# Layer a prepared while e waits, f's rows over the bfloat16 parts, and 32x32 blocks inverted on GpSimd in a six-layer decoder

## The reference, cut to what matters

```
x = norm(x + a(x))          # layer norm, q/k/v, rotation, 1+s+s*s/2 in place of exp, 16 heads of 16
x = norm(x + b(x, ctx))     # attention on ctx, with mask, bias
x = norm(x + c(x))          # 8 experts, top 2, 256 -> 512 -> 256
x = norm(x + d(x))          # delta rule in chunks, two causal filters (3 and 31 taps), a gate, a mix of four
x = norm(x + e(x, ctx))     # attention, softmax, without projections
x = norm(x + f(x))          # 256 -> 704 -> 256, inputs and weights rounded to 4-bit values by blocks of 16
```

## Time and profile before

| | |
|---|---|
| median of 3 runs (3577.76 to 3584.74) | 3583.84 us |
| profiled execution, its own time | 3585.07 us |
| profiled execution, span from first to last instruction | 3582.9 us |
| TensorE busy (weight loads) | 3074.0 us (2306.0) |
| VectorE busy | 2406.8 us |
| ScalarE busy | 1390.2 us |
| GpSimd busy | 355.2 us |
| mean granted clock of TensorE, share of full speed | 0.91 |

### The profile page before, as it was taken

How to read it: one execution, slowest core, us unless ns; L and a number is a source line. 1 busy time by engine, 2 the same in 40 slices (tenths; PEclk the granted TensorE clock), 3 DMA queues, 4 the chain that set the end, 5 groups by cost and what they waited for, 6 DMA issues and landing times.

```text
span 3582.9 us, 49503 instructions
## 1 busy us (share of the span) xinstructions
PE 3074.0 (86%) x18500; PEld 2306.0 (64%) x18500; DVE 2406.8 (67%) x5671; ACT 1390.2 (39%) x2889; POOL 355.2 (10%) x710
## 2 busy tenths in 40 slices
PE   4688889899898989989898998989899898999664
PEld 2466757677575766767576676757667675777452
DVE  5526567585866758577685767768576776867764
ACT  2334343434343343434344443344444334342321
POOL 1002001010100101001010100101010010101200
PEclk7789999998999999899999999999999999999776
DMA  3434234233323433332333333233433333341201
GB/s 103 88 87 104 54 89 95 69 84 86 84 57 77 104 72 82 83 86 60 77 85 91 72 89 86 64 77 87 89 72 86 86 67 77 80 97 50 48 12 24
DMA packets 592812, 275.92 MB, mean 77 GB/s; under 512 B 464808, under 2 KB 555072, under 8 KB 592576
## 3 DMA queue, kind: packets, MB, share of 16 engines
q1 hardware_dynamic: 490176, 138.53, 20.5%
q10 hardware_dynamic: 102400, 134.23, 12.1%
HBM read 156.55 MB, written 14.68 MB: 48 GB/s over the span
## 4 chain that ended last, share of the span: by engine, by line
PE 52%; DVE 23%; ACT 8%; issue 6%; DMA 5%; SPq 3%; POOL 3%; DVEq 0%; ACTq 0%; POOLq 0%
PE bank L890 20%; PE bank L1094 7%; PE bank L965 5%; PE bank L942 5%; ACT pt_f L1354 3%; DVE region L1971 3%; SPq L696 3%; DMA qT_f<-rest_f 2%; DVE nm_f L1711 2%; PE bank L1255 2%; PE bank L925 2%; PE bank L1176 2%; DMA kT_f<-split_f 2%; ACT split_f L1365 2%; PE bank L957 1%
## 5 line engine op out<-in xcount | busy, mean ns | idle before, releaser
L1354 ACT ACTIVATE pt_f<-bank 128x512 f32<-128x512 f32 x768 | 417.4, 596 | 368.5 <-PE bank L942 366.0
L1094 PE MATMUL bank<-c_w,c_hb 128*128 128x256 f32 x2048 | 509.2, 395 | 1.6 <-ACT c_hb L1483 0.3
L890 PE MATMUL bank<-xTc,c_w 128*128 128x256 f32 x2048 | 498.3, 393 | 1.3
L1711 DVE TENSOR_REDUCE nm_f<-bank 128x2 f32<-128x512 f32 x512 | 315.4, 685 | 203.1 <-PE bank L925 202.3
L1094 PEld LDWEIGHTS bank<-c_w,c_hb 128*128 128x128 f32 x2048 | 393.0, 200 | 64.9 <-ACT c_hb L1483 8.9
L890 PEld LDWEIGHTS bank<-xTc,c_w 128*128 128x128 f32 x2048 | 387.7, 195 | 64.8 <-issue 6.0
L1971 DVE SCALAR_TENSOR_TENSOR region<-vpad,cols,region 128x256 f32<-128x256 f32 x1024 | 425.8, 490 | 0.0
L942 PE MATMUL bank<-qT_f,kT_f 102*128 102x256 bf16 (+1 forms) x1536 | 293.9, 310 | 108.8 <-ACT pt_f L1354 39.4
L1483 ACT ACTIVATE c_hb<-bank,cols 128x256 f32<-128x256 f32 x512 | 213.8, 471 | 328.1 <-PE bank L890 328.0
L942 PEld LDWEIGHTS bank<-qT_f,kT_f 102*128 102x128 bf16 (+1 forms) x1536 | 123.6, 103 | 290.5 <-ACT pt_f L1354 120.9
L965 PE MATMUL bank<-pt_f,v_f 128*32 128x256 f32 x3072 | 231.5, 428 | 0.0
(11 more groups left out here) (309 smaller groups left out, 5012.4 us busy)
## 6 DMA issues: line engine op xcount, KB each, us to landing
c_w<-in_c_w ACTq DMA_DIRECT2D x256, 512.0 KB, 4.9
gram_scratch<-region SPq DMA_DIRECT2D x32, 256.0 KB, 2.3
x<-in_x SPq DMA_DIRECT2D x16, 256.0 KB, 5.7
x<-in_ctx SPq DMA_DIRECT2D x16, 256.0 KB, 5.9
ctxb<-in_ctx SPq DMA_DIRECT2D x16, 256.0 KB, 2.8
out_dram<-x SPq DMA_DIRECT2D x16, 256.0 KB, 2.2
qT_f<-split_f SPq DMA_TRANSPOSE x192, 3.3
kT_f<-split_f SPq DMA_TRANSPOSE x192, 3.4
```

The source lines that it names most:

```text
L890: mm = pe.matmul(out_ap, l, r, start=(i == 0), stop=(i == len(pairs) - 1))
L1094: mm = pe.matmul(PS[use][:, t * D:(t + 1) * D], c_hb[:, k, t * P:(t + 1) * P], c_w2[:, e % W_SLOTS, k, :], start=(k == 0), stop=(k == HC - 1))
L1354: act.activation(dst, PS[use].rearrange("p (c s) -> p c s", c=c), func, **kw).then_inc(*PS.drained(use))
L1711: dve.tensor_reduce(a.nm[:, :, h], PS[use].rearrange("p (t s) -> p t s", t=T), AX.X, ALU.max, negate=True)\
```

## The change

BASE goes from 4 to 5: blocks of 32x32, four in a matrix, 32 partitions, 31 pairs of operations, and doubling levels 5 and 6 alone. The orders of all engines are written anew. In a full step, layer a's norm and projection come before e's maxima, its v projection and first scores right after e's, its scores stand between f's segments, and the first doubling product (now d_one5) comes after a_out and b_in. f's inner rows move from pt into the tile split, over the bfloat16 parts, and f restores the constant columns of split when it is done; hence new waits: ScalarE waits for e's transposes before a's copies and for a's before f's tanh, and VectorE for x2 before f_res. Layer a's turned input gets a place of its own (aT = yf), the divided heads and the row maxima (on, mT, m3) move into slots of pt, and bank uses follow the new order.

```diff
-BASE = 4
+BASE = 5
...
-CONSTANTS = 54 - 4 * (LEVELS - 2)
+CONSTANTS = 30
...
-ONE = (["e_in"] + E_
-
-       + ["a_norm", "e_res", "a_proj", "e_apply", "f_in", "a_rope", "f_up0", "a_part1", "f_up1", "a_part2", "a_turnq",
-          "f_round0", "a_turnk", "f_round1", "f_down", "f_res", "f_apply"]
-       + A_[4:] + ["b_in", "b_ctx", "a_res", "a_apply", "b_x", "b_proj"]
-       + attention_segments("b", True) + ["b_res", "b_apply"])
+B_ = attention_segments("b", True)
+ONE = """
+a_load e_in e_part1 e_part2 e_turnq e_turnk a_norm a_proj a_rope e_max0 e_max1 e_max2 e_max3 e_shift a_part1 e_again a_part2
+""".split() + E_[10:-1] + """
+a_v a_turnq a_turnk e_out e_res e_apply f_in a_score0a a_score0b f_up0 a_score1a a_score1b f_up1 a_weigh0 a_score2a a_score2b
+a_weigh1 a_score3a a_score3b f_round0 a_weigh2 a_weigh3 f_round1 a_out b_in b_ctx a_res a_apply f_down b_x f_res b_proj
+""".split() + B_[:2] + ["f_apply"] + B_[2:] + ["b_res", "b_apply"]
...
     ("sync", None, """
-e_in e_turnq e_turnk e_again a_norm a_turnq d_blocks d_fetch a_turnk d_place d_begin f_apply b_turnq b_turnk b_again
+a_load e_in e_turnq e_turnk a_norm e_again a_turnq a_turnk d_blocks d_fetch d_place d_begin f_apply b_turnq b_turnk
+b_again
...
     ("gpsimd", None, """
-d_norm a_norm d_blocks e_res d_solve0 d_solve1 d_solve2 d_solve3 f_res a_res d_out d_res c_res b_res
+a_norm d_norm d_blocks e_res d_solve0 d_solve1 d_solve2 d_solve3 a_res f_res d_out d_res c_res b_res
...
     ("gpsimd", 17, """
-d_norm d_blocks d_solve0 d_solve1 d_solve2 d_solve3 e_res d_out f_res d_res
+d_norm d_blocks d_solve0 e_res d_solve1 d_solve2 d_solve3 f_res d_out d_res
...
     ("tensor", None, """
-d_in c_in c_gate d_proj c_comb c_up0a c_up0b e_max0 e_max1 c_down0a e_max2 e_max3 c_down0b c_up1a e_again c_up1b
-c_down1a e_score0a e_score0b e_score1a e_score1b e_weigh0 e_score2a c_down1b e_score2b e_weigh1 e_score3a d_token
-e_score3b e_weigh2 e_weigh3 e_out c_up2a c_up2b a_norm c_down2a c_down2b a_proj f_in c_up3a f_up0 f_up1 c_up3b d_chan
-c_down3a c_down3b d_gram c_up4a c_up4b f_round0 c_down4a f_round1 d_grams f_down a_score0a a_score0b a_score1a
-a_score1b a_weigh0 a_score2a c_down4b a_score2b a_weigh1 a_score3a c_up5a a_score3b a_weigh2 a_weigh3 d_one4 a_out
-b_in d_two4 b_ctx a_res d_twb4 c_up5b d_one5 b_x d_two5 b_proj c_down5a d_twb5 d_one6 c_down5b d_two6 c_up6a d_scan0
...
+d_in c_in d_proj a_norm a_proj c_gate e_max0 c_comb e_max1 c_up0a e_max2 c_up0b e_max3 c_down0a c_down0b e_again
+c_up1a c_up1b e_score0a c_down1a e_score0b c_down1b e_score1a c_up2a e_score1b e_weigh0 e_score2a e_score2b e_weigh1
+e_score3a d_token e_score3b e_weigh2 e_weigh3 a_v e_out c_up2b d_chan c_down2a c_down2b d_gram c_up3a f_in a_score0a
+d_grams a_score0b c_up3b f_up0 a_score1a c_down3a a_score1b c_down3b f_up1 c_up4a a_weigh0 a_score2a c_up4b a_score2b
+a_weigh1 a_score3a c_down4a a_score3b c_down4b f_round0 a_weigh2 a_weigh3 f_round1 c_up5a a_out b_in d_one5 b_ctx
+d_two5 a_res d_twb5 f_down d_one6 b_x c_up5b b_proj d_two6 c_down5a c_down5b d_scan0 c_up6a d_scan1 d_scan2 d_scan3
...
     ("vector", None, """
...
+e_part1 e_part2 a_norm a_proj a_rope d_proj c_gate e_max0 c_comb e_max1 e_max2 e_max3 e_shift a_part1 c_down0b d_conv
+d_silu d_token a_part2 c_down1b d_norm e_out e_res e_apply f_in d_gram c_down2b d_grams d_fir0 f_up0 d_fir1 d_fir2
+f_up1 c_down3b f_round0 f_round1 d_fir3 d_fir4 c_down4b d_one5 a_out d_fir5 d_two5 b_ctx a_res d_twb5 a_apply d_fir6
+f_res b_proj b_part1 b_part2 f_apply d_sums d_turn c_down5b b_max0 b_max1 b_max2 b_max3 b_shift c_down6b d_logit
...
-        low = region[0:P // 2, 2048:3072]
-        blkX, blkT, blkU = (low[:, i * 256:(i + 1) * 256].rearrange("p (r c) -> p r c", r=BB) for i in range(3))
-        blkT2 = low[:, 256:768]
-        blk_tmp = low[:, 768:832]
...
+        BN = 8 * NBK
+        square = lambda x: x[0:BN, 0:BB * BB].rearrange("p (r c) -> p r c", r=BB)
+        blkT, blkX = square(region[:, 2048:3072]), square(region[:, 3072 + 7 * 512:3072 + 9 * 512])
+        blkU = blkX
+        blk_tmp = wTn[0:BN].rearrange("p a s -> p (a s)")
...
-        f_h = flat_pt[:, 0:T * FF].rearrange("p (t n) -> p t n", t=T)
...
+        flat_split = at_.split[:, :, :, :, :].rearrange("p t i h x -> p (t i h x)").bitcast(F32)
+        f_h = flat_split[:, 0:T * FF].rearrange("p (t n) -> p t n", t=T)
...
                 for j in range(BB - 1):
-                    if j % 4 == 0:
-                        yield f"d_solve{j // 4}"
+                    if j % 8 == 0:
+                        yield f"d_solve{j // 8}"
...
                 act.wait_ge(*att["a"]["src"](b))
+                if b >= LAG["e"]:
+                    for half in range(HALVES):
+                        act.wait_ge(*att["e"][f"turned{half}"](b - LAG["e"]))
...
                     yield f"f_up{t}"
+                    if t == 0:
+                        if b + LAG["f"] < NB:
+                            for half in range(HALVES):
+                                act.wait_ge(*att["a"][f"turned{half}"](b + LAG["f"]))
...
                 yield "f_res"
+                if b + LAG["f"] < NB:
+                    dve.wait_ge(*xo["x2_ready"](b + LAG["f"]))
                 residual(b, "f_y", yf, x6)
+                dve.memset(a.split[:, :, 0, :, MASK0:MASK0 + 3], 1.0)
+                dve.memset(a.split[:, :, 0, :, MAX0:MAX0 + 3], 0.0)
+                dve.memset(a.split[:, :, :, :, SLOT:PITCH], 0.0)
+                dve.memset(a.split[:, :, 1, :, MAX0:MAX0 + 3], 1.0)
```

More of the change, by code:

```diff
@@ L155 @@
+a_weigh2 a_weigh3 a_out b_in b_ctx a_res b_x b_proj w_turn0 w_turn1 w_turn2 w_turn3 b_max0 b_max1 b_max2 b_max3
 b_again b_score0a b_score0b b_score1a b_score1b b_weigh0 b_score2a b_score2b b_weigh1 b_score3a b_score3b b_weigh2
@@ L192 @@
[L192 to L195 removed]
+e_part1 d_in e_part2 a_rope d_proj c_in c_gate c_comb c_up0a c_up0b a_part1 e_again a_part2 c_up1a c_up1b e_score0a
@@ L228 @@
-a_norm e_res a_proj e_apply f_in a_rope c_down2b d_norm d_gram f_up0 a_part1 f_up1 a_part2 f_round0 c_down3b f_round1
-d_grams d_fir0 d_fir1 f_res d_fir2 d_fir3 f_apply d_one4 d_fir4 a_out d_two4 b_ctx c_down4b a_res d_twb4 a_apply
-d_one5 d_fir5 b_proj d_two5 b_part1 d_twb5 b_part2 d_fir6 c_down5b b_max0 d_sums b_max1 b_max2 d_turn b_max3 b_shift
-c_down6b d_logit d_weight d_mix d_ms d_out d_res d_apply b_out c_down7b c_res c_apply b_res b_apply
+e_part1 e_part2 a_norm a_proj a_rope d_proj c_gate e_max0 c_comb e_max1 e_max2 e_max3 e_shift a_part1 c_down0b d_conv
@@ L257 @@
-f_up1 f_round0 d_turn f_round1 d_logit d_weight d_mix d_ms d_out f_res f_apply d_res d_apply
+e_part1 e_part2 d_proj d_conv d_silu d_token e_max0 d_norm e_max1 e_max2 e_max3 e_shift d_gram d_grams d_fir0 d_fir1
+d_fir2 d_fir3 e_out e_res e_apply f_in d_fir4 f_up0 f_up1 f_round0 f_round1 d_one5 d_fir5 d_two5 d_twb5 d_fir6 d_sums
+f_res f_apply d_turn d_logit d_weight d_mix d_ms d_out d_res d_apply
 """),
@@ L339, in at, with maxima, scores, turned_up @@
         u.extend((segment, use, bank) for use, bank in uses)
-    def attention(l, again):
-        if again:
-            for g in range(4):
-                at(f"{l}_max{g}", *((f"{l}_m{h}", h % 4) for h in range(4 * g, 4 * g + 4)))
-            at(f"{l}_again", (f"{l}_rT", 0))
-        for g in range(5):
-            if g < 4:
-                at(f"{l}_score{g}", *((f"{l}_s{h}", h % 2) for h in range(4 * g, 4 * g + 4)))
-            if g == 1 and not again:
-                at(f"{l}_weigh0", (f"{l}_sv", 3))
-            if g in (1, 3):
-                at(f"{l}_weigh{g - 1}", (f"{l}_o{g // 2}", 2 + g // 2))
-        at(f"{l}_out", (f"{l}_ot0", 0), (f"{l}_ot1", 1))
-    attention("e", True)
-    at("a_norm", ("a_hT", 2))
-    at("a_proj", ("a_qk0", 3), ("a_qk1", 0), ("a_v", 1))
-    at("f_in", ("f_xT", 2))
-    for t in range(T):
-        at(f"f_up{t}", (f"f_g{t}a", 0), (f"f_g{t}b", 1), (f"f_u{t}a", 2), (f"f_u{t}b", 3))
-    for t in range(T):
-        at(f"f_round{t}", (f"f_hT{t}a", 0), (f"f_hT{t}b", 1))
-    at("f_down", ("f_y", 2))
-    attention("a", False)
+    def maxima(l):
+        for g in range(4):
+            at(f"{l}_max{g}", *((f"{l}_m{h}", h % 4) for h in range(4 * g, 4 * g + 4)))
+    def scores(l, g):
+        at(f"{l}_score{g}", *((f"{l}_s{h}", h % 2) for h in range(4 * g, 4 * g + 4)))
+    def turned_up(t):
+        at(f"f_up{t}", (f"f_g{t}a", 0), (f"f_g{t}b", 1), (f"f_u{t}a", 2), (f"f_u{t}b", 3))
+    at("a_norm", ("a_hT", 0))
+    at("a_proj", ("a_qk0", 1), ("a_qk1", 2))
+    maxima("e")
+    at("e_again", ("e_rT", 0))
+    for g in range(4):
+        scores("e", g)
+        if g in (1, 3):
+            at(f"e_weigh{g - 1}", (f"e_o{g // 2}", 2 + g // 2))
+    at("a_v", ("a_v", 2))
+    at("e_out", ("e_ot0", 0), ("e_ot1", 1))
+    at("f_in", ("f_xT", 2))
+    scores("a", 0)
+    turned_up(0)
+    scores("a", 1)
+    turned_up(1)
+    at("a_weigh0", ("a_sv", 3), ("a_o0", 2))
+    scores("a", 2)
+    scores("a", 3)
+    at("f_round0", ("f_hT0a", 0), ("f_hT0b", 1))
+    at("a_weigh2", ("a_o1", 3))
```

(21 more changed lines are left out.)

186 lines of the change are left out of this document (93 added, 93 removed).

## The result

The changed kernel takes 3758.46 us (median of 4 runs, 3751.16 to 3765.53), the kernel before 3580.98 us beside it: ratio 1.0495, 95% interval 1.047 to 1.052. It is slower by 177 us; forecast were 118, with a range that holds the result. The profiled execution took 3760.71 us, its span 3759.0 us.

A forecast was written before the change was run, and what follows sets the result against it. TensorE's in-order list plus its waits was taken to bound a full step; +26.4 - 18.7 + 1.7 - 2 = +7.4 us, times 16 = 118, on 3585 gave 3703, said as 3700; the range took in 3515 and 3815.

The forecast's parts named there:

- The late inverse: First doubling product of layer d: GpSimd's longer inversion ends after TensorE arrives, which then waits 13 to 17 us each step.
- The stretch: From the gram product for A to the first doubling product: 60 us instead of 33.6, +26.4 a step.
- the formula: GpSimd's inversion priced by base time, slope per element and gaps: 35.7 us for 31 pairs, without VectorE's slowing.
- VectorE's presence: Slowing of GpSimd's 62 inversion operations by VectorE working beside them: 4 us, between 3 and 8.
- TensorE's list: TensorE's work between the gram product and the first doubling product in the new order: 43 to 47 us.
- -18.7 + 1.7 - 2: Per step: rest of the step -18.7 us, lower clock after the wait +1.7, idle filled by layer a's early products -2.
- 16 x 7.4: Whole kernel: layer d's 16 runs each lose a full step's 7.4 us, 118 us together.
- up to 15 us more: Item 15, step 17: e_res stands inside GpSimd's solve, which waits for it; counted as no more than the others.
- The fill of 2 us a step: Layer a's early products fill TensorE's idle time between e's maxima: 2 us a step, between none and 6.
- The solve was not hidden: Rival: TensorE reaches the doubling product after the inverse, no stall, -9.5 us a step, 3435 us; chance 0.12.
- The gaps were filled: Rival: chain at 55 us and early layer a giving back 8 us, -3.6 a step, 3525 us; chance 0.12.
- GpSimd held up for long: Rival: VectorE's tap runs hold GpSimd's solve, up to +16 us a step, 3950 us; sign operations over 2 us; chance 0.10.

The follow-up runs named there:

- inv32_old_order: The kernel before with 32x32 blocks alone and doubling level 4 out, old orders and places kept: 3896.3 us, ratio 1.0872.
- taps_late: The changed kernel with 20 of VectorE's 34 filter taps moved out of the inversion to later places: 3848.2 us, ratio 1.0737.
- inv16_old_tail: The changed kernel with 16x16 blocks and doubling level 4 back, and the old orders in steps 16 and 17: 3502.3 us, ratio 0.978.
- old_tail: The changed kernel with the old orders of all engines in steps 16 and 17 alone, without level 4's segments: 3741.9 us, ratio 1.0477.
- inv16_new_order: The changed kernel with its new orders and places, but 16x16 blocks and doubling level 4 back: 3547.2 us, ratio 0.9903.
- skip8: The changed kernel without pairs 8 to 15 of the inversion's 31, so part of the inverse is left out: 3596.4 us, ratio 1.0052.

## Why the prediction was right, and where it was not

**The late inverse: right, and shown.** The stretch was put at 60 us and is 61.9 in the step shown; its parts were forecast as 10.1, 39.7, 1.8 and 8.0 and are 7.9 (2269.3 to 2277.23), 43.6, 2.0 and 8.3. The slope taken from blocks of at most 64 elements held up to 256: in inv32_old_order with VectorE idle 87 elements took 0.32 and 0.33 us, in taps_late 256 took 0.61. (The Trainium skill, GPSIMD Engine Reference, "Elementwise — side-by-side cycle accounting", has 2.6 cycles an element, by which I estimated 2.2 ns; these rows give 1.7 between 87 and 256 elements of the multiplication. The subtraction, with VectorE idle, goes from 0.24 us at 31 elements to 0.72 at 256, 2.1 an element, which agrees. The rows decide.) The middle times of inv32_old_order's operations with VectorE idle, added up over the 31 pairs with the gaps, come to 35.7 us, the formula's value. Beside VectorE's work the formula's 31.1 us of operations are (604 + 642) x 31 = 38.6 us here:

```profile
L893 POOL TENSOR_TENSOR region<-region,wTn 32x31 f32<-32x31 f32 (+15 forms) x496 | 318.4, 642 | 38.9
L891 POOL TENSOR_TENSOR wTn<-region 32x31 f32<-32x31 f32 (+15 forms) x496 | 299.6, 604 | 210.5 <-DMA region<-gram_scratch 172.9
```

**The mis-sized terms.** VectorE's presence was taken as 4 us between 3 and 8; it is 43.6 - 35.7 = 7.9, the upper bound. I priced it by GpSimd's side alone. That it slows VectorE's taps in turn (0.40 to 0.75 us), and so f's gating, had no term: the prediction names a slowed VectorE, but only as holding back f's rounding inside a wait that is there anyway. It adds the 6.5 us wait at a_weigh0. The fetch's 10.1 was 7.9 and by luck made up for half. TensorE's list of 43 to 47 us was right where VectorE is left alone (44 in inv16_old_tail) and is 52 in the changed kernel, so the wait was 8 to 10 us and not 13 to 17. For the step this changed nothing, as the inverse ends the stretch either way: +28 against +26.4 for the stretch, 218.5 - 61.9 = 156.6 us for the rest against 210.2 - 33.6 = 176.6, which is -20.0 where the sum had -18.7 + 1.7 - 2 = -19.0. Per step +8.3 against +7.4.

**The step that failed: "16 x 7.4".** The count gave each of the last two items the full step's +7.4, 15 us together; they cost 73. Their stretches grew by (62.4 - 29.6) + (74.5 - 37.8) = 69.5 us, where 2 x 26.4 = 52.8 were counted. All other work behind item 13's product grew by 3.5 us in sum (18.7 more ahead of item 14's gram product, 13.3 and 1.9 less in the other two parts), where 2 x -19 = -38 was counted. The two misses, 16.7 and 41.5, are all of the 58 us by which the forecast was low; the first two items' 4 for 15 and the full steps' 99 for 89 cancel. What the count had at nothing were the orders that the change wrote anew: with them and the short inversion the last part is 63.5 us longer already, 41 of it by the entries of steps 16 and 17, and the long inversion adds 9.5. The prediction took the last steps for the same chain and looked at their orders for item 15's e_res alone, "up to 15 us more". That f's products wait for VectorE in front of the last doubling is seen in the trace, but old_tail has neither f_up1 nor f_round0 there and its stretches are as long, so it isn't the whole reason. That 3758 lies in the range is in part luck: the range was made wide for chains and holds in every step, and a third of the loss lies behind the full steps. The fill of 2 us a step could not be seen by itself.

**The rivals.** The solve was not hidden. The gaps were filled, by more than I gave them: inv16_new_order is 7.2 us a step faster than before with the same inversion. The break-even was put at a stretch of 52.6 us; skip8 has 52.3 and a step of 208.0 against 210.2, so it lies at 54 to 55 if the rest of the step stays. GpSimd held up for long came true only for one item, 8.70 us in the changed kernel's last solve, beside 30 taps. (The sign given for it, single operations over 2 us, is too wide: the norm's operation L877 takes 3.27 us in every full step.) The Trainium skill, SBUF — State Buffer, "Who interferes with whom", has the second engine block for the whole instruction of the first. The held operations stayed until the end of a run, many instructions longer than that; in the full steps the two alternate, which is nearer to it.

## What to carry to other kernels

Before a doubling level is handed to a slower engine, add up the chain to the point where the fast engine meets it again, and price the sharing on both sides: the engine that was not on the path became late and made TensorE wait elsewhere. Count the first and last steps of a pipeline by their own orders; here the new orders alone made the last part 63.5 us longer. Ask of every small job that stands behind the lengthened one on the same engine who waits for it: a norm did, twice. When moving a wait only makes the next one, as in five of the orders tried here, look for what is nearly as long as the stretch: here the inverse's chain took 62 us, TensorE's way to the product 52, and VectorE was busy for 56.
